# Reordering the drain of a windowed attention and top-1 expert kernel: output product, register reads, routing pieces, groups and unread products

## The reference, cut to what matters

```python
# attention, 16 heads of 16; windows of 128 tokens, plus every 32nd token as a global one
scores = 0 everywhere, q.k*scale inside a window, and added for pairs of global tokens
attn   = softmax(scores, axis=-1)           # over all 2048 keys: a zero score still counts exp(0)
x = layernorm(x + (attn @ v) @ wo.T + bo)
# top-1 of 8 experts, hidden width 64
top1 = argmax(x @ Wg.T);  xhat = normalised x
y    = sum over e of (top1 == e) * (gelu((xhat*ln_scale[e] + ln_bias[e]) @ W1[e] + b1[e]) @ W2[e] + b2[e])
out  = layernorm(x + y)
```

## Time and profile before

| what | us |
|---|---|
| median of 3 runs | 399.14 |
| lowest and highest of the 3 | 398.56 and 401.33 |
| the profiled execution's own time | 401.99 |
| its span, first to last instruction | 400.2 |
| PE busy | 342.2 |
| DVE busy | 284.2 |
| ACT busy | 226.9 |
| POOL busy | 201.5 |

### The profile page before, as it was taken

The page is one execution under the profiler, slowest core; times in us unless marked ns, Lnnn a source line. Parts: engine busy times, 40 slices in busy tenths (PEclk is TensorE's granted clock), DMA queues, the critical chain, the costliest instruction groups (busy, mean ns, idle before and its releaser), DMA issues.

```text
span 400.2 us, 12415 instructions
## 1 busy us (share of the span) xinstructions
PE 342.2 (85%) x4438; PEld 284.0 (71%) x4438; DVE 284.2 (71%) x829; ACT 226.9 (57%) x521; POOL 201.5 (50%) x352
## 2 busy tenths in 40 slices
PE   4989899999999999999989999988775798999400
PEld 3858688887887888887868888776453786877300
DVE  7795547676567675777888778796968796788810
ACT  3325476655665566556658866656653444777620
POOL 5243133443553435434447877844854343376772
PEclk9999999999999999999999999999999688999855
DMA  8762662100000000001013212100113554563220
GB/s 236 227 208 70 207 199 85 28 2 26 26 1 26 7 20 26 4 28 28 2 29 70 85 51 91 43 16 2 72 44 100 152 198 127 152 206 107 87 83 0
DMA packets 27981, 31.74 MB, mean 79 GB/s; under 512 B 5183, under 2 KB 25882, under 8 KB 27931
## 3 DMA queue, kind: packets, MB, share of 16 engines
q1 hardware_dynamic: 20246, 18.22, 15.9%
q0 software_dynamic: 3456, 8.66, 5.9%
q10 hardware_dynamic: 4230, 4.22, 3.2%
HBM read 20.96 MB, written 11.17 MB: 80 GB/s over the span
## 4 chain that ended last, share of the span: by engine, by line
PE 54%; DVE 24%; issue 7%; ACT 7%; POOL 3%; DMA 2%; SPq 0%; POOLq 0%; DVEq 0%; ACTq 0%
DVE row_max_t L1186 13%; PE ps L1436 8%; PE ps L1473 8%; PE ps L1398 7%; PE ps L1428 6%; PE ps L1703 5%; PE ps L1456 4%; PE ps L1721 3%; ACT probs L896 3%; PE ps L1450 3%; POOL out_dram L719 2%; PE ps L1420 2%; PE ps L1689 2%; PE ps L1440 2%; ACT boundsT_t L907 2%
## 5 line engine op out<-in xcount | busy, mean ns | idle before, releaser
L896 ACT ACTIVATE probs<-ps 128x1024 f32<-128x1024 f32 x64 | 62.1, 1022 | 59.9 <-PE ps L1440 59.7
L1186 DVE TENSOR_REDUCE row_max_t<-ps 128x16 f32<-128x2048 f32 x31 | 70.9, 2286 | 21.5 <-PE ps L1428 21.4
L1436 PE MATMUL ps<-q_slots,k_slots 32*128 32x256 f32 x512 | 40.5, 400 | 10.2 <-DVE row_max_t L1186 9.1
L663 POOL TENSOR_TENSOR attn_t<-num_t,rden_t 128x256 f32<-128x256 f32 x32 | 19.9, 621 | 54.1 <-DVE rden_t L1215 54.0
L746 ACT ACTIVATE pvT_t<-ps 128x512 f32<-128x512 f32 x34 | 20.3, 598 | 38.6 <-PE ps L1450 35.8
L646 POOL TENSOR_TENSOR bounds_t<-guard_t,bounds_t 128x16 f32<-128x16 f32 x32 | 7.1, 222 | 68.8 <-DVE guard_t L1197 68.7
L1428 PE MATMUL ps<-k_slots,q_slots 32*128 32x128 f32 x1056 | 38.7, 283 | 3.0 <-DVE dg L1037 1.3
L1428 PEld LDWEIGHTS ps<-k_slots,q_slots 32*128 32x128 f32 x1056 | 32.5, 186 | 8.9 <-issue 6.0
L719 POOL DMA_INDIRECT out_dram<-other_tiles x32 | 31.5, 985 | 11.7 <-issue 7.0
L907 ACT ACTIVATE boundsT_t<-ps,head_mask 128x128 fp32r<-128x128 f32 x128 | 36.7, 381 | 0.9 <-PE ps L1619 0.7
L620 POOL DMA_INDIRECT sorted_rows<-rows,place_i x32 | 31.7, 990 | 10.1 <-issue 6.3
(11 more groups left out here) (278 smaller groups left out, 796.9 us busy)
## 6 DMA issues: line engine op xcount, KB each, us to landing
table<-rest_sums SPq DMA_DIRECT2D x4, 1088.0 KB, 6.1
other_tiles<-sorted_rows SPq DMA_DIRECT2D x32, 136.0 KB, 2.4
xs<-in_L_attn_x_dram SPq DMA_DIRECT2D x16, 256.0 KB, 2.7
rows<-in_L_attn_x_dram ACTq DMA_DIRECT2D x4, 1024.0 KB, 7.4
sorted_rows<-pad_rows SPq DMA_DIRECT2D x9, 136.0 KB, 1.8
first_tiles<-sorted_rows SPq DMA_DIRECT2D x8, 136.0 KB, 2.1
w<-in_L_ffn_W_dram SPq DMA_DIRECT2D x2, 256.0 KB, 8.2
w<-in_L_ffn_W_dram SPq DMA_DIRECT2D x1, 512.0 KB
```

Source lines behind the costliest of these rows:

```text
L896: act.activation(probs[:, 2 * h:2 * h + 2, :], ps[:, 2 * h:2 * h + 2, :], ACT.Exp).then_inc(probs_ready, 1)
L1186: dve.tensor_reduce(row_max[:], ps_all, op=ALU.max, axis=AX.X).then_inc(max_ready, 1)
L1436: mm(ps[:, u, 2 * c * P:(2 * c + 2) * P], k_slots[quad(u), s, c, :], q_slots[quad(u), s, c, :, :].rearrange("p a n -> p (a n)"), start=Tru ...
```

## The change

On TensorE, `turn_tiles(0)` moves from behind `weigh` to the end of step 33, and with it the wait for the first list and the reading of pair 0's registers. Pairs begin one step later (PAIRS_FROM is NW + 2), so the last output product, in step 34, stands ahead of pair 0. In `pair_steps(i)` the registers of pair i+1 are read right behind `first_layer(i)`, ahead of `turn_hidden(i-1)`, except for pair 8, whose registers are still read at its start, since they need the second list. `keep_busy(n)` issues n products of bf16 ones and zeros, 512 columns wide, into a PSUM bank whose content is not read: 4, 4 and 3 of them in step 33 and 6 each in steps 34 and 35. ScalarE's copies for the pairs move with them, and the scaling of windows 30 and 31 goes behind pair 2 instead of 3.

On VectorE `route` is cut in two (the second half is `choose`); for batch 0 the halves lie in steps 18 and 19, `find_places(0)` moves from step 19 to 20, and the 15 steps of `factors(0)` from steps 20 and 21 to steps 21, 22 and 23. `hidden_constants`, `select_parts` and `scale_first_layer` move to steps 16, 25, and 24 and 25. `list_tiles(1)` moves from behind pair 0 to behind pair 1 and its `normalise(0)`. The scaling and scattering of batch 0 begin two steps later, and window 22's and 23's rows are scattered in step 31 with three others. GROUPS has seven groups in place of six.

```diff
-        RANKS_AT = (19, 27, 33, 35)
-        PAIRS_FROM = NW + 1
-        SCALED_AT = {22: (0, 5), 23: (5, 10), 24: (10, 16), 29: (16, 20), 30: (20, 24), 35: (24, 30)}
-        SCATTERED_AT = {23: (0, 2, 3), 24: (3, 5, 6), 25: (6, 8, 9), 26: (9, 11, 12), 27: (12, 14, 15), 28: (15, 16, 16),
-                        30: (16, 19, 20), 31: (20, 22, 23), 32: (23, 24, 24)}
-        FACTORS_DONE = {22: 1, 29: 2, 35: 3}
+        RANKS_AT = (20, 27, 33, 35)
+        PAIRS_FROM = NW + 2
+        SCALED_AT = {24: (0, 5), 25: (5, 10), 26: (10, 16), 29: (16, 20), 30: (20, 24), 34: (24, 30)}
+        SCATTERED_AT = {25: (0, 2, 3), 26: (3, 5, 6), 27: (6, 8, 9), 28: (9, 11, 12), 29: (12, 14, 15), 30: (15, 18, 19),
+                        31: (19, 22, 24)}
+        FACTORS_DONE = {24: 1, 29: 2, 34: 3}
...
-        GROUPS = ((0, 2), (2, 6), (6, 10), (10, 14), (14, 18), (18, 20))
+        GROUPS = ((0, 2), (2, 4), (4, 8), (8, 12), (12, 16), (16, 18), (18, 20))
...
@@ block.scalar @@
-                if i == 3:
+                if i == 2:
                     act.wait_ge(ln_ready, NB)
...
-                if not steady and t > PAIRS_FROM:
-                    pair_steps(t - PAIRS_FROM - 1)
+                if not steady and t == PAIRS_FROM:
+                    keep_tiles(0)
+                if not steady and t >= PAIRS_FROM:
+                    pair_steps(t - PAIRS_FROM)
...
@@ block.vector: within_steps @@
+                if t == 19:
+                    choose(0)
                 if t == 21:
-                    factors(0, 9, FACTOR_STEPS)
+                    factors(0, 0, 4)
                 if t == 23:
+                    factors(0, 10, FACTOR_STEPS)
+                if t == 25:
                     select_parts()
-                if t == 25:
-                    hidden_constants()
@@ block.vector: between_steps @@
+                if t == 16:
+                    hidden_constants()
                 if t == 18:
                     route(0)
-                if t == 19:
+                if t == 20:
                     find_places(0)
-                if t == 20:
-                    factors(0, 0, 9)
-                if t in (21, 22):
-                    scale_first_layer(t - 21)
+                if t == 21:
+                    factors(0, 4, 6)
+                if t == 22:
+                    factors(0, 6, 10)
+                if t in (24, 25):
+                    scale_first_layer(t - 24)
...
                 finish(i)
-                if i == 0:
-                    list_tiles(1)
                 for g, (a, b) in enumerate(GROUPS):
                     if b == i + 1:
                         normalise(g)
+                if i == 1:
+                    list_tiles(1)
@@ block.tensor @@
+            def keep_busy(n):
+
+                for k in range(n):
+                    mm(ps_kv, own_wide[:, 0, :], own_wide[:, 0:4, :].rearrange("p e n -> p (e n)"), start=True, stop=True)
...
-                if not steady and t == PAIRS_FROM:
-                    turn_tiles(0)
...
+                if not steady and t == PAIRS_FROM - 1:
+                    pe.wait_ge(late_const, 19)
+                    pe.wait_ge(first_bias_taken, 1)
+                    keep_busy(4)
                 if pp:
                     pe.wait_ge(pvT_ready, t - 1)
                     turn_sums().then_inc(sums_in_psum, 1)
...
                     output_product(t - 3)
+                if not steady and t == PAIRS_FROM - 1:
+                    keep_busy(4)
...
+                if not steady and t == PAIRS_FROM - 1:
+                    turn_tiles(0)
+                    pe.wait_ge(lists_ready, 1)
+                    held[0] = experts_of(0)
+                    keep_busy(3)
                 if not steady and t >= PAIRS_FROM:
                     pair_steps(t - PAIRS_FROM)
+                    keep_busy(6)
...
-                if 2 * i in (0, TILES[0]):
-                    pe.wait_ge(lists_ready, 1 + (i > 0))
-                held[i] = experts_of(i)
+                if 2 * i == TILES[0]:
+                    pe.wait_ge(lists_ready, 2)
+                    held[i] = experts_of(i)
                 first_layer(i, held[i])
+                if i + 1 < PAIRS and 2 * (i + 1) != TILES[0]:
+                    held[i + 1] = experts_of(i + 1)
                 if i > 0:
                     turn_hidden(i - 1)
                 if i + 1 < PAIRS:
```

More of the change, by code:

```diff
@@ L320, in windowed_attention_then_top1_experts @@
         late_dve = sem("late_dve")
+        first_bias_taken = sem("first_bias_taken")
         table_zero = sem("table_zero")
@@ L883, in step @@
                     values_of(t + 1, (s + 1) % SLOTS, False)
-                if not steady and t == PAIRS_FROM:
-                    keep_tiles(0)
                 if not steady and t in SCALED_AT:
@@ L913, in _ @@
             attention_steps(act, step, first=0)
-            for i in range(NW + 3 - PAIRS_FROM, PAIRS):
+            for i in range(NW + 4 - PAIRS_FROM, PAIRS):
                 pair_steps(i)
@@ L1101, in route, with choose @@
                 link(dve.tensor_tensor(hit[:, part, :], zc[:, part, :], zmax[:, 0, part].unsqueeze(2).broadcast_to(per_expert), ALU.is_equal))
+            def choose(b):
+                first, end = BATCHES[b]
+                n = end - first
+                part = slice(first, end)
+                per_expert = [P, n, EXPERTS]
                 link(dve.tensor_tensor(hit[:, part, :], hit[:, part, :], rank[:].unsqueeze(1).broadcast_to(per_expert), ALU.mult))
@@ L1264, in between_steps @@
             def between_steps(t):
+                if t == 16:
+                    hidden_constants()
                 if t == 18:
                     route(0)
-                if t == 19:
+                if t == 20:
                     find_places(0)
-                if t == 20:
-                    factors(0, 0, 9)
-                if t in (21, 22):
-                    scale_first_layer(t - 21)
+                if t == 21:
[4 more added lines that the diff above has]
+                    scale_first_layer(t - 24)
                 if t == 26:
                     route(1)
+                    choose(1)
                 if t == 27:
@@ L1288, in between_steps @@
                     route(2)
+                    choose(2)
                     mark_tiles(0)
@@ L1295, in between_steps @@
                     route(3)
+                    choose(3)
                 if t == 35:
@@ L1345, in fold_first_bias @@
                 dve.wait_ge(ld_b, 48)
-                link(dve.tensor_tensor(b1_own[:], ps_kv[0:3 * EXPERTS, :].rearrange("r (e h) -> r e h", h=EH),
-                                       own[0:3 * EXPERTS, :].unsqueeze(2).broadcast_to([3 * EXPERTS, EXPERTS, EH]), ALU.mult))
+                dve.tensor_tensor(b1_own[:], ps_kv[0:3 * EXPERTS, :].rearrange("r (e h) -> r e h", h=EH),
+                                  own[0:3 * EXPERTS, :].unsqueeze(2).broadcast_to([3 * EXPERTS, EXPERTS, EH]), ALU.mult).then_inc(first_bias_taken, 1)
+                dve.wait_ge(first_bias_taken, 1)
                 link(dve.tensor_reduce(b_t[:, 0, :], b1_own[:].rearrange("r e h -> r h e"), op=ALU.add, axis=AX.X))
```

## The result

The changed kernel takes 409.12 us (median of 4 runs, 408.57 to 409.63) where the kernel before, on the same chip, takes 399.98 (4 runs, 398.56 to 401.33): a ratio of 1.0229, interval 1.0185 to 1.0273. It is slower by 2.3%; whether by more than 2% the interval leaves open. The prediction of 406.7 us was made against 399.14; as a ratio it is 1.019. The profiled execution of the changed kernel took 409.31, with a span of 407.6. Medians and ratios in this document are of fast executions: left out are one of e12 (560.37 us at a mean granted clock of 0.564; with it the median would be 395.85) and three of the kernel before beside e5 to e8 (405.49 to 406.57).

The account below looks back on a forecast made before the run. The prediction took TensorE's order of work and waits as the bound, its sequencer setting the pairs' 2.81 us pace. Slower pairs +8.8 and routing -1.2 gave +7.6 on the 399.14 median: 406.7 us, range 398 to 413.

Parts of the forecast that it names:

- parts 1 and 3: Pair loop: reads ahead of the transposes slow the pace from 2.81 to 3.65 us; pairs 9 to 19 end +8.8.
- the second stretch: Pairs 9 to 19, after the second list: pair 19 starts at 378.95 instead of 370.17, +8.8 us.
- Case A: Pair loop: TensorE's queue hides the reads, pace stays 2.81, kernel faster at 393.8 us; chance 0.15.
- case B: Pair loop: reads half hidden, pace near 3.3, full routing gain, 401 us, within 1%; chance 0.13.
- part 2: Drain: last output product ends near 311.0 instead of 313.46, routing 1.7 us sooner; five slower pairs eat the gain.
- the routing's 1.2 us: Attention steps: smaller routing pieces gain 1.5 us, a second scatter in step 31 costs 0.3; net -1.2.
- case D: Drain: the clock falls nevertheless, output product 31 takes 1.93 again; +1 to +2, 408 us; forecast including it 0.64.
- case C: Pair stretch: gaps opened by the reads let the clock fall, +1.4 for each pair met, 413 us; chance 0.08.
- parts 4 and 5: Tail: seven groups gain nothing at the old pace, pass on pair 19's delay at the new; attention steps: routing net -1.2.

Follow-up runs that it names:

- e12: e8 with the runtime bounds check of each register read left out, the list of experts being clamped where it is made; 395.13 us, ratio 0.9858.
- e5: e1 without the 23 unread products; 401.73 us, ratio 1.0012 to the kernel before.
- e8: e1 with the registers of pairs 1 and 2 read ahead, behind the preceding pair's first layer, as in the change; 396.66 us, ratio 0.9882.
- e1: Changed kernel with the register reads back at the pair's start (pair 0's stay in step 33); 397.15 us, ratio 0.9918 to the kernel before.
- e2: Kernel before with only the reads moved: pair i+1's registers read behind first_layer(i); 412.29 us, ratio 1.0302.
- e6: Changed kernel with only one of a pair's two reads ahead of turn_hidden, the other behind the second layer; 399.43 us, ratio 0.9931.
- e7: Kernel before with each pair's two registers read twice at the pair's start; 423.15 us, ratio 1.0577.
- e4: Changed kernel without the 23 unread products; 410.23 us, ratio 1.0246 to the kernel before.
- e10: e8 with the six layernorm groups of the kernel before in place of seven; 396.86 us, ratio 0.9897.
- e11: Changed kernel with batch 0's routing put back as it was before; 411.29 us, ratio 1.0277 to the kernel before.
- e13: e12 with the second tile list made behind pair 0, as in the kernel before; 394.29 us, ratio 0.9809.

## Why the prediction was right

**The pace (parts 1 and 3).** It was worked out as 3.65 and is 3.66; the second stretch was to cost +8.8 and costs 36.60 - 28.04 + 0.36 = 8.9 from pair 8 on. Each link of the loop is found in the trace: counted from the first address step (341.22), the reads go from 0.74 to 2.18 us, where 0.75 to 2.05 was worked out, the transposes start at 2.23 (2.15) and the copy ends at 3.71 (3.61). e1 and e2 show that it is the reads' place, e6 that it is the reads' length. The sequencer as the setter of 2.80 was read from a gap of 0.2 us; e7 shows it right, with 1.34 us more for two more reads. The Trainium skill (TensorE: Matmul & The Clock Gate, Architectural detail) gives TensorE's queue as 64 deep. No run here shows its depth; the traces show that it doesn't help here, as what stood behind a read in the program didn't start before the read's end (343.40 and 343.45 in the pair above). Case A, which was to follow from that rule, and case B are refuted by the pace.

**The drain (part 2).** Its times were worked out without the routing's 1.2 us, which the sum takes off at the end. With these 1.2 off, they stand against the trace so: output product 31 ended at 309.8, measured 309.44; last ranks at 312.7, measured 312.81; pair 3 at 320.2, measured 320.27; the second list at 330.8, measured 329.75; pair 8 at 337.6, measured 337.62. That some agree to 0.1 us is luck: the changed kernel's execution was 0.3 us later already at window 15 (152.61 against 152.30), ahead of everything that the prediction counts. VectorE's idle time of 1.67 us, which was to be the whole gain, is gone. The list was worked out 1 us too late, with no effect, since pair 8 waited for nothing but its turn.

**The last step, from span to time.** This is where the 2.4 us between 406.7 and 409.12 lie. The sum on spans was +7.6 and is +7.4. It was then put on the median, 399.14 + 7.6. But the profiled execution of the kernel before, at 401.99, lay 2.0 above the median later measured (399.98), and that of the changed kernel only 0.2 above its own (409.31, 409.12): between the medians the change costs 9.1. So the difference of two profiled executions understates the change by 1.8, and the median of three runs was 0.8 low. The times of the kernel before differ more from run to run (398.56 to 401.33) than those of the changed one (408.57 to 409.63). The mean granted clock goes along with that: of the 19 executions of the kernel before beside e5 to e8, the six up to 400.61 us had 0.957 to 0.970, the five above 404 us 0.938 to 0.945. That the difference lies in the stretches at 0.50 in the drain is argued, not shown. So the forecast's mechanism was right on the spans to 0.2 us, and what was off was the base to which it was added.

**The unread products.** They were priced at 0.21 each by the row of a 64-column product, which is 0.19: no row gave the 0.21 for 512 columns, it was a choice between the two bounds. Six of them took 1.46 us from the first start to the last end, and one alone 0.38, so they were 0.22 apart. That they cost nothing is in keeping with e4, where taking them out saved nothing, but the prediction gave them no worth either except as the opposite of case D. Their worth of 3.8 us shows only in e1 against e5. Case D, that the clock falls in the drain all the same, didn't occur. Nor did case C: the clock stayed at 1.00 until 385.6, past TensorE's last product (381.63 + 1.12 = 382.75), though TensorE idled 0.9 us in each pair. The rule of the Trainium skill (same page, Loop structure matters more than you think), that waits between bursts cool the clock, agrees with e4 and e5, where the drain's waits go with stretches at 0.50, and with e7, whose pairs, 4.14 us apart with longer waits, lost the full clock from 367.31 to 374.14; it doesn't with the changed kernel's pairs, where TensorE waits as well and the granted clock stays at 1.00. So case C stood nearer than the changed kernel's trace alone suggests.

**Groups and routing (parts 4 and 5).** Seven groups are worth nothing (e10). The routing pieces were to give 1.5 us and give 1.7 by e11; at window 31 the whole change has the same 1.7 (from the row maximum of window 15 to that of window 31). The second scatter in step 31, which was to cost 0.3 us, did hold up GpSimd's multiplication (timeline of GpSimd in the changed kernel, to compare with the earlier trace rows):

```profile
292.88 0.96 POOL L621 DMA_INDIRECT sorted_rows<-rows,place_i  x1 [0.30 <-issue]
293.87 0.63 POOL L664 TENSOR_TENSOR attn_t<-num_t,rden_t 128x256 f32<-128x256 f32 x1
```

VectorE's `rden_t` was ready at 292.86 + 0.26 = 293.12, 1.4 us earlier than before (294.48), but the multiplication started only 0.8 earlier, right behind the scatter. It had started 0.19 us behind `rden_t` before and starts 0.75 behind it now, so the scatter costs it 0.56 us. Little of that reached the chain: VectorE's next addition is still 1.3 us earlier (298.06 against 299.37), where the one before had been 1.4 (292.38 against 293.76).

**What stays open.** How the 0.8% that all parts but the reads gain (e1) is split: the routing's 1.7 us and the unread products' 3.8 us were measured in different kernels, and together they are more than e1's 3.3. So the rest of the drain's new order seems to cost some 2 us: without the unread products e5 starts pair 8 0.7 us later than the kernel before, though it has the routing's gain. The list behind pair 1 is a part of that, by e13; the others were not told apart. The place of the output product was not tried alone.

## What to carry to other kernels

In this kernel a register read on TensorE's sequencer (0.65 us) held back everything behind it in the program. Put such a read where the instructions already queued last longer than the read, here behind the second layer, and not ahead of the work that the loop through another engine needs first, here the transposes for ScalarE's copy. Reading ahead gains only if the read itself leaves the loop. Count the sequencer's sum for each iteration as a limit of its own (here 2.80 us, where 2.62 was reached with a shorter sum), and shorten it first, by leaving out the bounds check where the data is clamped. Before you keep a clock up with filler work, see what bounds the stretch behind it: the same 23 products were worth 3.8 us with one order of the reads, and 0.7 us or nothing with the other.

## What the runs showed of the hardware that was not expected

- The bounds check is 40% of a read: two checked reads took 1.40 us from the first load to the next wait (348.97 to 350.37 in the kernel before), two unchecked ones 0.84 (350.06 to 350.90 in e12).
- The profile put 14.3 us of TensorE's idle time, in 17 pieces, down to a ScalarE operation that had ended 0.6 us before TensorE went on. The releaser was the sequencer. In e7 the same kind of wait is called "issue". The sign is that the named operation's end and the start behind it don't meet.
- At a granted clock of 0.50 the busy share says the opposite of progress: in the stretch from 337.18 the kernel before is busy for 3.41 us of 3.41 with 15 products, the changed one in nearly the same stretch for 2.40 of 3.40 with 19.
